# Four reorderings around the attention of a two-layer network: values made like keys, an earlier store, a later product

## The reference

```
x = x + gated_conv(_ln_c(x));  t = tokens(x)
t = t + mixture_of_experts(_ln_t(t));  x = from_tokens(t)
x = x + attention(_ln_c(x));  t = tokens(x)
t = t + soft_mixture(_ln_t(t));  x = from_tokens(t)
```

```
k = softmax(Wk x + bk, over points);  q = softmax(Wq x + bq, over the 16 dimensions)
v = Wv x + bv
context = einsum('bdn,ben->bde', k, v);  out = einsum('bhdn,bde->bhen', q, context)
x = x + Wo out + bo
```

## Time and profile before

| | before |
|---|---|
| median of 3 runs | 220.24 us (217.92 to 221.53) |
| profiled execution | 219.29 us, of which the span of its instructions is 217.4 us |
| TensorE busy | 191.6 us, 88% |
| VectorE busy | 140.8 us, 65% |
| ScalarE busy | 110.2 us, 51% |
| POOL busy | 73.9 us, 34% |
| granted TensorE clock, mean | 0.894 of 2.4 GHz |

### The profile page before, as it was taken

The page is one execution under the profiler, slowest core; times in us unless marked ns, Lnnn a source line. Parts: engine busy times, 40 slices in busy tenths (PEclk is TensorE's granted clock), DMA queues, the critical chain, the costliest instruction groups (busy, mean ns, idle before and its releaser), DMA issues.

```text
span 217.4 us, 3515 instructions
## 1 busy us (share of the span) xinstructions
PE 191.6 (88%) x1281; PEld 84.5 (39%) x1281; DVE 140.8 (65%) x310; ACT 110.2 (51%) x182; POOL 73.9 (34%) x105
## 2 busy tenths in 40 slices
PE   6987878979899999999999899786969899999880
PEld 4315543266244232222245788332224354323120
DVE  2448779758658858888867948853355057474862
ACT  2198579203687864561047548624762655454000
POOL 7550194340670222333380575870304600000000
PEclk9999555557999999999999859999996799999998
DMA  6519256000000000000000000000000000202022
GB/s 181 141 51 136 44 161 252 0 3 0 0 0 5 0 3 0 0 3 0 0 0 5 0 0 3 0 3 0 2 0 0 0 3 0 51 0 51 2 48 48
DMA packets 5761, 6.50 MB, mean 30 GB/s; under 512 B 2008, under 2 KB 5368, under 8 KB 5616
## 3 DMA queue, kind: packets, MB, share of 16 engines
q1 hardware_dynamic: 5024, 5.62, 10.2%
q10 hardware_dynamic: 720, 0.66, 1.3%
HBM read 4.01 MB, written 1.05 MB: 23 GB/s over the span
## 4 chain that ended last, share of the span: by engine, by line
PE 59%; DVE 16%; ACT 10%; issue 6%; DMA 4%; POOL 2%; SPq 1%; DVEq 0%; ACTq 0%
PE ps L882 7%; PE ps L715 6%; PE ps L380 5%; PE ps L666 5%; PE ps L927 5%; PE ps L914 4%; PE ps L365 3%; DMA hidden_of_all_tokens<-hidden_of_all_tokens 3%; PE ps L772 2%; PE ps L587 2%; ACT hidden_of_all_tokens L390 2%; PE ps L431 2%; ACT hidden_of_all_tokens L1089 2%; PE ps L685 2%; DMA x_resid<-in_x 2%
## 5 line engine op out<-in xcount | busy, mean ns | idle before, releaser
L1678 DVE SCALAR_TENSOR_TENSOR gated_x<-ps,bn_shift_negated,hidden_of_all_tokens 128x512 f32<-128x512 f32 x32 | 22.5, 745 | 18.1 <-PE ps L917 17.7
L1185 ACT ACTIVATE hidden_of_all_tokens<-ps,bn_shift,bn_scale 128x512 f32<-128x512 f32 x32 | 23.1, 773 | 15.5 <-PE ps L882 15.5
L390 ACT ACTIVATE hidden_of_all_tokens<-ps,weights 128x512 f32<-128x512 f32 x16 | 10.9, 682 | 28.5 <-PE ps L380 27.8
L384 POOL TENSOR_TENSOR hidden_of_all_tokens<-hidden_of_all_tokens 128x512 f32<-128x512 f32 x16 | 17.8, 1122 | 20.9 <-DVE hidden_of_all_tokens L402 16.9
L1089 ACT ACTIVATE hidden_of_all_tokens<-ps,weights 128x512 f32<-128x512 f32 x32 | 19.9, 685 | 9.1 <-PE ps L666 8.9
L1530 DVE TENSOR_TENSOR hidden_of_all_tokens<-hidden_of_all_tokens,ps 128x512 f32<-128x512 f32 x32 | 20.5, 682 | 5.8 <-PE ps L685 5.7
L882 PE MATMUL ps<-x_normed,weights 64*64 64x512 f32 x128 | 22.3, 664 | 0.5 <-ACT hidden_of_all_tokens L1185 0.5
L409 DVE TENSOR_TENSOR x_normed<-hidden_of_all_tokens 128x512 f32<-128x512 f32 x16 | 11.3, 707 | 14.0 <-ACT hidden_of_all_tokens L392 13.8
L380 PE MATMUL ps<-hidden_of_all_tokens,weights 128*128 128x512 f32 x32 | 16.9, 627 | 1.8 <-POOL hidden_of_all_tokens L384 1.8
L927 PE MATMUL ps<-gated_x,weights 64*64 64x512 f32 x32 | 16.5, 595 | 2.0 <-DVE x_resid L1686 1.4
L666 PE MATMUL ps<-x_normed,weights 64*64 64x512 f32 x128 | 17.4, 612 | 1.0 <-ACT hidden_of_all_tokens L1089 1.0
(11 more groups left out here) (286 smaller groups left out, 399.6 us busy)
## 6 DMA issues: line engine op xcount, KB each, us to landing
weights<-in_weights SPq DMA_DIRECT2D x1, 2087.5 KB, 7.8
out_x<-x_resid SPq DMA_DIRECT2D x8, 128.0 KB, 2.4
hidden_of_all_tokens<-hidden_of_all_tokens SPq DMA_DIRECT2D x7, 128.0 KB, 3.8
x_resid<-in_x ACTq DMA_DIRECT2D x4, 128.0 KB, 3.3
x_resid<-in_x SPq DMA_DIRECT2D x4, 128.0 KB, 3.7
weights<-in_weights SPq DMA_DIRECT2D x1, 419.0 KB, 5.3
taps_shifted<-taps_padded SPq DMA_DIRECT2D x9, 18.1 KB
weights<-in_weights SPq DMA_DIRECT2D x1, 130.0 KB, 2.4
```

The lines of the kernel that those rows point to most:

```text
L384: pool.tensor_tensor(SQ[:, cols(q)], XC[:, cols(q)], XC[:, cols(q)], ALU.mult).then_inc(sq_ready, 1)
L1185: act.activation(h1_tile(t), tile_of(t, Z1_BANK), ACT.Relu, bias=bn_c[:, p:p + 1], scale=bn_a[:, p:p + 1]).then_inc(h1_ready, 1)
L1678: dve.scalar_tensor_tensor(HW[:, t % PAIRS].rearrange("p (b n) -> p b n", n=N), tile_of(t, Z2_BANK).rearrange("p (b n) -> p b n", n=N), ne ...
```

## The change

Values are now made as keys are: the weight's other 32 columns are the stationary operand, and groups of four products of 256 columns fill bank 3, once behind the second and once behind the fourth pair of key products. ScalarE copies that bank to `V_ROWS` ahead of the second key exponential, TensorE turns it in four turns into bank 2, and ScalarE copies that to `V`, whose blocks now stand in the order of the turned keys' blocks. The second queries move from behind the third to behind the second pair of keys. The second query exponential moves behind the key copies, and the third behind the contexts' copy. VectorE scales the second half of the keys right behind the first. The eighth `queries_store` stands ahead of the first root of the fourth norm, and the first square of that norm ahead of the last `queries_norm` on POOL. The third up stands behind the turn of the logits, with two `keep_clock` products behind it, which first wait for the fourth norm's last Ln.

```diff
+        V_ROWS = SW[:, 0:Q]
...
                 if q % 2:
                     last.then_inc(k_ready, 1)
-                if q == 2:
+                    pe.wait_ge(ln_taken, 3 * NQ)
+                    for j in range(4):
+                        last = pe.matmul(PS[cols(j, 32), 3, cols(q // 2, N)], w("wkv", cols=slice(32, 64)), T[:, cols(2 * q - 2 + j, N)], start=True, stop=True)
+                if q == 1:
                     queries(1)
-            pe.wait_ge(ln_taken, 3 * NQ)
-            for t in range(16):
-                last = pe.matmul(PS[:, 3, cols(t, 32)], T[:, cols(t, P)], w("wkv", cols=slice(32, 64)), start=True, stop=True)
+            last.then_inc(v_ready, 1)
+            pe.wait_ge(v_out, 1)
+            for k in range(4):
+                last = pe.transpose(PS[:, 2, cols(k, P)], V_ROWS[:, cols(k, P)], w("ident"))
             last.then_inc(v_ready, 1)
...
-            pe.wait_ge(v_out, 1)
+            pe.wait_ge(v_out, 2)
             pe.wait_ge(kt_out, 2)
...
-                    last = pe.matmul(PS[0:32, 2, cols(b, 32)], V[:, cols(2 * b + jj, 32)], KT[:, cols(4 * (2 * g + jj) + j, 32)], start=jj == 0, stop=jj == 1)
+                    last = pe.matmul(PS[0:32, 2, cols(b, 32)], V[:, cols(4 * (2 * g + jj) + j, 32)], KT[:, cols(4 * (2 * g + jj) + j, 32)], start=jj == 0, stop=jj == 1)
...
             f_route(3).then_inc(fl_ready, 1)
-            f_up(2)
             pe.wait_ge(fl_chain, 1)
...
             last.then_inc(fl_ready, 1)
+            f_up(2)
+            pe.wait_ge(ln_taken, 4 * NQ)
+            keep_clock(pe, WT, 3, 2)
...
             queries_out(1)
+            act.wait_ge(v_ready, 1)
+            act.activation(V_ROWS, PS[:, 3], ACT.Copy).then_inc(v_out, 1)
             keys_exp(1)
             queries_exp(0)
             queries_out(2)
-            queries_exp(1)
-            act.wait_ge(v_ready, 1)
-            act.activation(V[:, :], PS[:, 3], ACT.Copy).then_inc(v_out, 1)
+            act.wait_ge(v_ready, 2)
+            act.activation(V[:, :], PS[:, 2], ACT.Copy).then_inc(v_out, 1)
             keys_out(0)
             keys_out(1)
+            queries_exp(1)
             queries_out(3)
-            queries_exp(2)
             act.wait_ge(cx_ready, 1)
...
+            queries_exp(2)
             queries_store(0)
...
             queries_store(6)
+            queries_store(7)
             ln_act_rstd(act, 3, 0, 1)
-            queries_store(7)
...
             keys_scale(0)
+            keys_scale(1)
             queries_max(1)
             queries_sum(0)
-            keys_scale(1)
...
+            ln_pool_square(pool, 3, 0)
             queries_norm(BH - 1)
-            for u in range(NQ):
+            for u in range(1, NQ):
                 ln_pool_square(pool, 3, u)
```

## The result

The changed kernel takes 211.76 us (median of 4 runs, 210.68 to 214.12) against 220.4 us: ratio 0.963, 95% interval 0.952 to 0.974. It is faster by more than 2%. The ratio leaves out one slow run of each kernel (214.12 and 221.53), so it is not the ratio of the medians. The forecast was 211.6 us. The profiled execution took 211.94 us, 7.35 less than the profiled one of before.

The account below looks back on a forecast made before the run. TensorE, busy 88% of the span with two late half-clock stretches, was taken as the bound. Gains 3.3 + 1.9 + 0.5 + 2.9 = 8.6 from 219.29 give 210.7; 0.95 profile-to-median distance makes 211.6 us, range 209.7 to 216.4.

Parts of the forecast that it names:

- Part 1: Attention stage: values made like keys and turned, keys' scalings together; head blocks start 3.3 us earlier.
- Part 2: End of attention: eighth store ahead of first root, first square ahead of last normalising; third variance 1.9 us earlier.
- Part 3: Router softmax: third up and two dummy products behind the logits' turn; whole softmax chain 0.5 us earlier.
- The price for missing cover: Softmax stretch, third up behind the logits' turn: if the cover is missing, at most 0.5 us is lost.
- Part 4: Second slow stretch, after the router softmax: TensorE has more work, the clock holds, 2.9 us won.
- The sum: Whole kernel: gains of 3.3, 1.9, 0.5 and 2.9 us add to 8.6 us.
- Rival (a): Behind the contexts in attention: clock falls once more, costing 3.4 us, total 215.0 us; chance 0.28.
- (b): Softmax stretch still loses the clock, the 2.9 us are not won, 214.5 us; chance 0.14 alone.
- (c): Clock falls behind the contexts and does not return before the feed-forward; slower, 223.9 us; chance 0.05.
- (d): POOL's 16 operations in attention already bound it, so nothing of 3.3 us comes; 214.9 us; chance 0.05.

Follow-up runs that it names:

- experiment 1: Changed kernel with values made token block by token block, keys' scalings apart and ScalarE's order, all as before: 213.43 us, ratio 0.977.
- experiment 6: Kernel before with eight dummy products of 256 columns among its sixteen value products: median 220.67 us against 219.19.
- experiment 2: Changed kernel with the eighth query store back behind the first root and the first square behind the last normalising: 214.24 us, ratio 0.978.
- experiment 5: Changed kernel without its two dummy products, third up still behind the logits' turn, second look: 217.28 us (one run).
- experiment 3: Changed kernel with the third up back ahead of the logits' turn and no dummy products: 217.55 us, ratio 0.994.
- experiment 7: Kernel before with only the new making of values, keys' scalings together and ScalarE's new order: 216.02 us against 219.19.
- experiment 4: Changed kernel without its two dummy products, third up still behind the logits' turn, first look: 214.43 us.
- experiment 8: Changed kernel with three dummy products of 256 columns in TensorE's waits around the contexts: 211.39 us.
- experiment 9: Changed kernel with the second query maximum ahead of both key scalings on VectorE: 210.65 us.
- experiment 11: Changed kernel with the second key scaling back behind the second query maximum and first query sum on VectorE: 213.79 us (one run).

## Why the prediction was right, point by point

- **Part 1, 3.3 us: measured 3.51** in the pair of profiles, and the same position, 11.69, in part 1 alone. The chain was named rightly: the head blocks wait for POOL and the third sum, not for the contexts. Contexts were priced at 0.95 and take 1.20; the slack hid it. One row was misread: the router's 0.64 us in the earlier trace rows is one group of four products, two records each, and not two groups. As 0.5 us was taken for a group all the same, and a group takes 0.55 up to the next product, this cost only 0.1. Experiments 1 and 6 add what the walk did not separate: by estimate most of this gain is the fall of the clock that it avoids, 2.6 us in the profile of before, and with a fall of 3.4 us in the place of 6.9 the part was worth 2.05. The walk took the fall of the profile for granted.
- **Part 2, 1.9 us: 2.10**, of which by positions the store has 1.5 and the square 0.6 (experiment 2).
- **Part 3, 0.5 us: 0.47.** The price for missing cover, "at most 0.5 us", was wrong if it means the dummies: without them experiment 5 lost 3.65 us by the sixth up, through the clock (51.76 against 48.11).
- **Part 4, 2.9 us: 2.48.** The term is over-sized by one step of the walk: the Relus of the fifth up start when the whole up is done, not when its first half is; ScalarE waits 0.51 us for it at 164.11. That the softmax stretch would keep its clock was right, and with the order as before it fell again (experiments 3, 6 and 7, for 10.3, 7.0 and 6.5 us). Taken away in experiment 3, parts 3 and 4 together cost 4.23 us by the sixth up, where they had won 2.95, because that fall was longer.
- **The sum, 8.6 us: 8.56.** That the median came to 211.76 owes something to chance: the 0.95 us added for the distance of the profile from the median is no property of the change. The profiled execution lies above its median, not below, and what filled the place of the 0.95 in it is the 1.23 us later start. The range was uneven in the same way: its lower end leaves the 0.95 out, its upper end has it in. The code ahead of the first queries is the same in all kernels, yet they stand anywhere between 114.34 and 117.99 us in the thirteen profiles counted.
- **Rival (a)**, a fall behind the contexts, is real: it is there in 2 of the 6 profiles that have part 1 as the change makes it (experiments 2 and 4). Its price was over-sized: 3.4 to 3.6 us long instead of 6.9, it costs 1.5 us (first variance at 27.50 against 25.98) and not 3.4.
- The Trainium skill, TensorE: Matmul & The Clock Gate, Part 4 (PE-mode transpose), says that turns do not count as busy for the clock as products do. The two falls of rival (a) would agree with it, but four of the six profiles have the same turns and kept 1.00, the changed kernel's among them; and as the same stretch has the contexts' 32-column products and waits, no run here separates them.
- **Rivals (b), (c), (d)** did not come: the softmax stretch held in every profile with the whole part 3, no fall behind the contexts lasted, and POOL's chain moved forward with the rest.

What stays open is why a fall lasts 3.4, 7, 10 or 14 us in one execution or another, and whether experiment 8's dummies make the contexts safe. Open too is how much the change wins over an execution of the kernel before whose clock held: one took 213.87 us at a mean granted clock of 0.931, by an estimate some 29 us at half clock in place of the 46 of the profiled one (twice the missing share of the clock, times the span), and no trace shows which of its falls were missing.

## What to carry to other kernels

Look at the granted clock by stretches beside the busy time: here TensorE was shown 100% busy for 3.8 us and lost half its clock right behind it. What an order costs through the clock can be more than the time of its own products: the third part puts work into a wait, and without it 4.2 us were lost by the sixth up. Before moving one instruction up, walk the whole chain of the other engines: here a scaling of 0.35 us had to move with the values, and with the scaling in its old place most of their gain was gone in the one execution that was run. Where executions differ by the clock in an untouched part, compare positions counted from a common instruction, not totals.

## What the runs showed of the hardware

- **A small VectorE instruction can cost three times its length beside POOL.** The scaling of 128 by 256 takes 0.35 us when POOL is idle, and 1.18 or 1.23 us when a POOL instruction begins within 0.03 us of it (experiments 9 and 11); in both it ends 0.15 us behind POOL's. In experiment 9 it starts 0.03 us behind POOL's, in experiment 11 it is shown 0.02 us ahead. The Trainium skill, SBUF — State Buffer, section Who interferes with whom, says that when VectorE runs in a mode that takes two ports, it and GpSimd contend, and whichever issues first has the shared pair of ports for its whole instruction while the other is blocked. Experiment 9 agrees; in experiment 11 the starts in the profile do not tell which was issued first, and no run shows in which mode the scaling ran.
- **The same order keeps the clock in one execution and loses it in the next** (experiments 4 and 5: 1.00 throughout the softmax stretch, and 0.52 for 14.1 us from within it), so a single profile says little on whether a filler is needed.
